# A mixture-of-experts audio tower on one core: the token embedding computed one round ahead, and the value product moved to other PSUM banks

## The reference

```python
# tokenizer: patches of 16 frames, stride 8, x 16 features -> 256; then layernorm with gamma, beta
y = einsum('bpi,di->bpd', patches, W) + b
h = (y - mean) * rsqrt(var + 1e-5) * gamma + beta
# attention on layernorm(h), one head of 256, 124 tokens per sequence, 128 sequences
h = h + softmax((q @ k.T) / scale) @ v
# experts on layernorm(h): router of 6 experts, the best two of each token, gates from a softmax over both
h = h + sum_k gate_k * expert_k(layernorm(h))      # three layers of 256 x 256, relu, relu, none
```

## Time and profile before

| | |
|---|---|
| time, median of 3 runs | 1345.66 us (1345.2 to 1346.94) |
| time of the profiled execution | 1342.78 us |
| its span, first to last instruction | 1341.0 us |
| mean granted TensorE clock | 0.967 |
| busy: PE, weight load, DVE, ACT, POOL | 1234.8, 1078.0, 1062.5, 838.0, 928.3 us |
| part A, until the last round's places | 0 to about 670 us |
| transition | about 670 to 700 us |
| part B | about 700 to 1341 us |

### The profile page before, as it was taken

How to read it: one execution, slowest core, us unless ns; L and a number is a source line. 1 busy time by engine, 2 the same in 40 slices (tenths; PEclk the granted TensorE clock), 3 DMA queues, 4 the chain that set the end, 5 groups by cost and what they waited for, 6 DMA issues and landing times. The chain is left out here.

```text
span 1341.0 us, 28426 instructions
## 1 busy us (share of the span) xinstructions
PE 1234.8 (92%) x7888; PEld 1078.0 (80%) x7888; DVE 1062.5 (79%) x3590; ACT 838.0 (62%) x1838; POOL 928.3 (69%) x740
## 2 busy tenths in 40 slices
PE   3899999999999999999629999999999999999994
PEld 3788888888888888887428788888888888888883
DVE  3589989998999899987547778787787787777873
ACT  1477666766676667766316666766667667666662
POOL 2127778777877787777753677676676676766766
PEclk7899999999999999999759999999999999999997
DMA  2124555544444444445677796667876778778755
GB/s 83 31 63 130 147 131 150 142 115 113 117 124 116 114 116 124 116 114 161 174 204 198 159 225 113 123 122 146 193 120 113 126 154 178 129 146 191 122 63 60
DMA packets 134564, 176.50 MB, mean 132 GB/s; under 512 B 38019, under 2 KB 102406, under 8 KB 134406
## 3 DMA queue, kind: packets, MB, share of 16 engines
q0 software_dynamic: 75456, 69.19, 32.7%
q1 hardware_dynamic: 56822, 101.44, 24.8%
q10 hardware_dynamic: 2128, 4.05, 1.0%
HBM read 168.72 MB, written 101.48 MB: 202 GB/s over the span
## 5 line engine op out<-in xcount | busy, mean ns | idle before, releaser
L533 POOL DMA_INDIRECT out<-yo,tail x268 | 438.7, 1637 | 199.3 <-issue 147.7
L481 POOL DMA_INDIRECT expert_rows<-rec,row_i x256 | 347.6, 1358 | 78.4 <-issue 64.2
L909 ACT ACTIVATE h2v<-bank,small 128x512 f32<-128x512 f32 x134 | 92.4, 690 | 206.9 <-PE bank L725 191.9
L749 PE MATMUL bank<-w_sb,h_hi 128*128 128x256 f32 x1072 | 208.7, 288 | 2.0 <-issue 2.0
L725 PE MATMUL bank<-x_hi,w_sb 128*128 128x512 f32 x536 | 178.2, 393 | 6.3 <-issue 2.7
L725 PE MATMUL bank<-h_hi,w_sb 128*128 128x512 f32 x536 | 177.0, 391 | 1.2 <-DVE h_lo L1229 1.2
L749 PEld LDWEIGHTS bank<-w_sb,h_hi 128*128 128x128 f32 x1072 | 171.3, 191 | 2.8 <-issue 2.7
L749 PE MATMUL bank<-w_sb,h_lo 128*128 128x256 f32 x536 | 151.4, 283 | 0.0
L868 ACT ACTIVATE xn<-h,nmr,rstd 124x256 f32<-124x256 f32 x128 | 66.4, 589 | 126.0 <-DVE nmr L1082 126.0
L725 PEld LDWEIGHTS bank<-x_hi,w_sb 128*128 128x128 f32 x536 | 101.3, 189 | 30.3 <-issue 7.3
L469 POOL TENSOR_TENSOR rstd<-vareps,neghalf 124x4 f32<-124x4 f32 x96 | 114.5, 1192 | 8.0
(11 more groups left out here) (187 smaller groups left out, 3115.0 us busy)
## 6 DMA issues: line engine op xcount, KB each, us to landing
w_sb<-split_weights SPq DMA_DIRECT2D x201, 512.0 KB
xg<-expert_rows SPq DMA_DIRECT2D x67, 530.0 KB
out<-h SPq DMA_DIRECT2D x32, 496.0 KB
small<-in_esmall SPq DMA_DIRECT2D x69, 134.0 KB
split_weights<-half_w SPq DMA_DIRECT2D x36, 256.0 KB
x_in<-in_x SPq DMA_DIRECT2D x32, 250.0 KB
raw_w<-in_eweights SPq DMA_DIRECT2D x36, 128.0 KB
out<-yo,tail POOLq DMA_INDIRECT x268
```

The source lines that it names most:

```text
L481: pool.indirect_dma_start(rows_dram, bass.IndirectOffsetOnAxis(ap=row_i[0:TOK, slot, j, k:k + 1], axis=0), rec[0:TOK, slot, j, :], None).t ...
L533: pool.indirect_dma_start(out, bass.IndirectOffsetOnAxis(ap=tail[:, s, j, E8:].bitcast(I32), axis=0), yo[:, ys, j, :], None, compute_op=AL ...
L749: mm = pe.matmul(banks[6 + b][:, (j % 2) * D:(j % 2 + 1) * D], act[:, c, j * P:(j + 1) * P], w[:, 2, c, wh, :], start=(c == 0 and p == 0), ...
L909: act.activation(h2v[:, m, :], banks[4 + m][:], ACT.Relu, bias=small[:, slot, DC + m:DC + m + 1]).then_inc(S["h2_v"], 1)
```

## The change

It moves stages by a round, and PSUM banks:

* Two rounds, -2 and -1, stand ahead of round 0. The split of the input (xT_hi, xT_lo) is now of group it + 2, and the embedding (PE), its statistics 0 and y (DVE) and their inverse standard deviation (POOL) are of group it + 1. h, statistics 1 and all behind keep their round.
* On ACT the split stands between gexp and qT, on DVE ahead of the weight chunk's lower half. On DVE statistics 0 stand behind nmr of x0, and y behind statistics 2. Input loads go three rounds ahead.
* The value product goes to banks 4 and 3 instead of 6 and 7; waits for banks follow.
* On POOL the power for statistics 1 comes first, then scatters 5 and 6, the power for statistics 0, scatter 7, the power for statistics 2, scatters 0 to 4.
* `fold()` runs on DVE at the end of round 0; PE keeps it behind the embedding, which in round 0 is now that of group 1. The upper and lower halves of the v weights move likewise.
* The constants of POOL are reordered: the two large clears (pad_rows, xg) come last, and the engines wait for smaller counts.

```diff
-            for it in range(G + DEPTH - 1):
+            for it in range(-2, G + DEPTH - 1):
...
-                if it + 1 < G:
-                    load_x(it + 1, (slot_it + 1) % RING)
+                if 2 <= it + 3 < G:
+                    load_x(it + 3)
+                if it < 0:
+                    return
...
@@ gpsimd, step @@
-                if x0:
-                    wait_apart(pool, S["ln1"], g * LN1_N + 2 * GB, S["pool_passed"])
-                    inverse_std(0, S["rstd1"], g)
-                if x5:
-                    scatter(x5[0], range(4, 6))
                 if x0:
                     wait_apart(pool, S["ln1"], g * LN1_N + 6 * GB, S["pool_passed"])
                     inverse_std(1, S["rstd2"], g)
                 if x5:
-                    scatter(x5[0], range(6, 8))
+                    scatter(x5[0], range(5, 7))
+                if xa:
+                    wait_apart(pool, S["ln1"], g * LN1_N + 2 * GB, S["pool_passed"])
+                    inverse_std(0, S["rstd1"], g)
+                if x5:
+                    scatter(x5[0], range(7, 8))
...
-                    scatter(g, range(4 if g < G - 1 else GB * TOPK))
+                    scatter(g, range(5 if g < G - 1 else GB * TOPK))
@@ tensor @@
-            pe.wait_ge(S["pool_const"], 20)
+            pe.wait_ge(S["pool_const"], 16)
...
-                if x0:
-                    g, slot, rnd = x0
+                if xa:
+                    g, slot, rnd = xa
                     pe.wait_ge(S["xT_high"], g + 1)
                     pe.wait_ge(S["xT_low"], g + 1)
...
-                        bank_read(pe, (S["v_ready"], it - 2, (it - 2) * 2 + pair + 1),
-                                  (S["ln1"], it - 1, (it - 1) * LN1_N + 2 * GB + 2 + 2 * pair))
+                        bank_read(pe, (S["ln1"], g - 1, (g - 1) * LN1_N + 2 * GB + 2 + 2 * pair))
...
-                            into = banks[6 + pair][0:TOK, j * D:(j + 1) * D]
+                            into = banks[4 - pair][0:TOK, j * D:(j + 1) * D]
@@ scalar @@
-            act.wait_ge(S["pool_const"], 20)
+            act.wait_ge(S["pool_const"], 2)
...
-                if x0:
-                    act.activation(xT_hi[:], x_in[:, slot, :], ACT.Identity).then_inc(S["xT_high"], 1)
...
                     act.activation(gexp[0:TOK, :], gap[0:TOK, :], ACT.Exp).then_inc(S["gate_exp"], 1)
+                if xs:
+                    wait(act, S["tok_ps"], g * 2)
+                    wait(act, S["xT_low"], g)
+                    act.activation(xT_hi[:], x_in[:, slot, :], ACT.Identity).then_inc(S["xT_high"], 1)
@@ vector @@
-                if x0:
-                    v.tensor_tensor(xT_lo[:], x_in[:, slot, :], xT_hi[:].bitcast(F32), ALU.subtract
-                                    ).then_inc(S["xT_low"], 1)
                 if x4:
                     probabilities(*x4)
...
-                    statistics(0, lambda j: embedded(j), S["ln1"], g * LN1_N, g)
...
-                        v.scalar_tensor_tensor(out=y[R, j, :], in0=embedded(j), scalar=mv[R, 0, j, 0:1],
-                                               in1=gamma_bc[R, :], op0=ALU.subtract, op1=ALU.mult).then_inc(S["ln1"], 1)
...
+                if xs:
+                    v.tensor_tensor(xT_lo[:], x_in[:, slot, :], xT_hi[:].bitcast(F32), ALU.subtract
+                                    ).then_inc(S["xT_low"], 1)
                     v.wait_ge(S["w_high"], it + 1)
...
                     v.scalar_tensor_tensor(out=nmr[R, 0, :], in0=mv[R, 1, :, 0], scalar=-1.0, in1=rstd[R, 1, :],
+                if xa:
+                    statistics(0, lambda j: embedded(j), S["ln1"], g * LN1_N, g)
 ...
+                if xa:
+                    for j in range(GB):
+                        v.scalar_tensor_tensor(out=y[R, j, :], in0=embedded(j), scalar=mv[R, 0, j, 0:1],
+                                               in1=gamma_bc[R, :], op0=ALU.subtract, op1=ALU.mult).then_inc(S["ln1"], 1)
+                if it == 0:
+                    fold()
+                    low_halves("v", 4)
                 if x3:
                     shifted_logits(*x3)
```

More of the change, by code:

```diff
@@ L485, in step @@
             def step(it, group_of):
[L486 to L492 removed]
+                xa, x0, x2, x4, x5 = (group_of(s) for s in (-1, 0, 2, 4, 5))
                 if x0:
@@ L578, in step @@
             def step(it, group_of):
-                x0, x1, x2, x3, x4 = (group_of(s) for s in range(DEPTH))
+                xa, x1, x2, x3, x4 = (group_of(s) for s in (-1, 1, 2, 3, 4))
+                if it == 1:
+                    pe.wait_ge(S["bv_ready"], 1)
                 if x1:
@@ L695, in step @@
                     g, slot, rnd = x1
+                    if it == 1:
+                        pe.wait_ge(S["folded"], 3)
                     for pair in range(2):
-                        bank_read(pe, (S["ln1"], it, it * LN1_N + 2 * GB + 2 + 2 * pair),
-                                  (S["v_ready"], it - 2, (it - 2) * 2 + pair + 1))
+                        if pair == 0:
+                            bank_read(pe, (S["pT_sb"], it - 2, it - 1))
+                        else:
+                            bank_read(pe, (S["pos"], it - 4, (it - 4) * POS_N + 1), (S["xn2T_sb"], it - 3, (it - 3) * 2 + 1),
+                                      (S["v_ready"], it - 2, (it - 2) * 2 + 2))
                         for j in (0, 1):
                             b = 2 * pair + j
-                            into = banks[6 + pair][0:TOK, j * D:(j + 1) * D]
+                            into = banks[4 - pair][0:TOK, j * D:(j + 1) * D]
                             for c in range(DC):
@@ L789, in step @@
             def step(it, group_of):
-                x0, x1, x2, x3, x4 = (group_of(s) for s in range(DEPTH))
-                if x0:
[L792 to L795, removed]
-                    act.activation(xT_hi[:], x_in[:, slot, :], ACT.Identity).then_inc(S["xT_high"], 1)
[L797 to L801, removed]
+                xs, x0, x1, x2, x3, x4 = (group_of(s) for s in (-2, 0, 1, 2, 3, 4))
                 if x4:
@@ L856, in step @@
                     act.activation(rhT[:], banks[5][:, 0:GT], ACT.Relu, bias=rb1_col[:, 0:1]).then_inc(S["rh_sb"], 1)
[L858 to L861, removed]
+                if it >= 0:
+                    slot_it, rnd_it = slot_of(it, group_of)
+                    act.wait_ge(raw_loaded[slot_it], rnd_it * 16 + 16)
+                    wait(act, w_stored[slot_it], rnd_it * 16)
+                    act.activation(half_w[:, slot_it, 0, :], raw_w[:, slot_it, :], ACT.Identity).then_inc(S["w_high"], 1)
                 if x0:
@@ L870, in step @@
                                        ).then_inc(S["xn1_ready"], 1)
+                if it == 0:
+                    act.wait_ge(S["const_loaded"], N_CONST)
+                    high_halves("v")
+                    act.wait_ge(S["fold_sb"], 9)
+                    act.activation(proj["q"][:, 0, :, :], qk_raw[:], ACT.Identity).then_inc(S["proj_high"], 1)
                 if x1:
@@ L875, in step @@
                         act.activation(v_sb[0:TOK, 2 * pair:2 * pair + 2, :],
-                                       banks[6 + pair][0:TOK, :].rearrange("p (b n) -> p b n", b=2),
+                                       banks[4 - pair][0:TOK, :].rearrange("p (b n) -> p b n", b=2),
                                        ACT.Identity).then_inc(S["v_ready"], 1)
@@ L985, in step @@
             def step(it, group_of):
-                x0, x1, x2, x3, x4 = (group_of(s) for s in range(DEPTH))
-                if x0:
-                    g, slot, rnd = x0
-                    v.wait_ge(S["xT_high"], g + 1)
-                    v.tensor_tensor(xT_lo[:], x_in[:, slot, :], xT_hi[:].bitcast(F32), ALU.subtract
-                                    ).then_inc(S["xT_low"], 1)
+                xs, xa, x0, x1, x2, x3, x4 = (group_of(s) for s in range(-2, DEPTH))
                 if x4:
@@ L1073, in step @@
                     v.reciprocal(rinv[R, :], probs[R, :, TOK]).then_inc(S["av"], 1)
[L1075 to L1078, removed]
+                if xs:
+                    g, slot, rnd = xs
+                    v.wait_ge(S["xT_high"], g + 1)
+                    v.tensor_tensor(xT_lo[:], x_in[:, slot, :], xT_hi[:].bitcast(F32), ALU.subtract
+                                    ).then_inc(S["xT_low"], 1)
+                if it >= 0:
+                    slot_it, rnd_it = slot_of(it, group_of)
+                    v.wait_ge(S["w_high"], it + 1)
+                    v.tensor_tensor(half_w[:, slot_it, 1, :], raw_w[:, slot_it, :], half_w[:, slot_it, 0, :].bitcast(F32),
+                                    ALU.subtract).then_inc(S["w_low"], 1)
                 if x0:
@@ L1094, in step @@
                     statistics(2, lambda j: h[R, g % KEPT, j, :], S["av"], at + 1 + GB, g)
+                if xa:
+                    g, slot, rnd = xa
+                    at = g * LN1_N
+                    if it == -1:
```

(13 more changed lines are left out.)

60 lines of the change are left out of this document (27 added, 33 removed).

## The result

| | before | after |
|---|---|---|
| median of 20 runs each | 1345.33 us | 1338.81 us |
| ratio of times (95% interval) | | 0.995 (0.994 to 0.996) |
| profiled execution: time, span | 1342.78, 1341.0 us | 1336.13, 1334.3 us |
| mean granted TensorE clock | 0.967 | 0.969 |

A forecast was written before the change was run, and what follows sets the result against it. A DVE-POOL ring through rstd was taken to hold the 19.11 us round, then one through ACT's half_w; 4.9 from part A's rounds plus 6.0 from the head made 10.9 us gained, 1335 us forecast, range 1316 to 1346.

The forecast's parts named there:

- The round: Rounds 4 to 30 of part A, lshift to lshift: 18.99 us after the change, against 19.11 before.
- the ring as written: Path from lshift through ACT's half_w, DVE's half_w, statistics 0 and y to the next lshift: 18.99 us.
- Round 31: Round without embedding, statistics 0 and y after the change; PE idles 2.11 us before rec's transposes; 16.9 us.
- The head: Start of the kernel up to lshift of round 3: 79.2 instead of 85.25, 6.0 us gained (bounds 3 and 8).
- Behind part A: POOL's closing chain of scatters and DVE's tables shift with round 33; nothing gained or lost there.
- DVE is the only bound: Full rounds: half_w's ring shorter than read, DVE's own work gives 18.36 us a round, 1318 in all; chance 0.12.
- POOL becomes the bound: Full rounds: slower powers and scatters lift POOL from 17.8 to 19.6 us a round, 1351 in all; chance 0.07.
- nothing gained: Rounds and head: a ring of 19.2 and a fold delaying q lose the gain; 1342 to 1347 us; chance 0.13.
- the clock falls each round: Full rounds: an unbroken PE pause lowers its clock, costing 1.2 to 1.9 us each; 1370 to 1385; chance 0.05.

The follow-up runs named there:

- half_act_early: The changed kernel with ACT's half of the weight chunk (half_w) between qT and pT instead of behind rhT; 1306.89 us.
- half_dve_late: The changed kernel with DVE's half of half_w behind y instead of ahead of nmr, ACT untouched; 1314.21 us.
- before_half_early: Control: the kernel before the change, with ACT's half_w moved between qT and pT; 1345.83 us.
- fold_first: The changed kernel with the weight fusing (fold) back ahead of the first h on PE, DVE and ACT; 1337.24 us.
- xt_behind_logits: The changed kernel with ACT's half_w between qT and pT and, from round 3, DVE's xT_lo between lshift and psums; 1300.64 us.
- value_banks_67: The changed kernel with the value product back in banks 6 and 7, its waits adapted; 1483.11 us in one run.

## Why the prediction was right, and where it was not

* **The round: right.** 18.99 was forecast and 18.99 to 19.00 came, by the ring as written, with ACT's half_w at L + 11.28 and DVE's waits of 0.72 and 0.30 (0.65 and 0.3 forecast). half_act_early and half_dve_late open it, and before_half_early shows that it is the change's own.
* **Round 31: off by 0.5, by the path as written.** It took 17.37, for 16.9. PE idles ahead of the transposes of rec, but for 3.52 and not 2.11, behind which the granted clock is 0.57 (599 to 603); DVE comes to half_w at L + 13.30, for 12.92. With 27 rounds of 19.006 that makes the 4.0 gained of 4.9.

```profile
597.85 0.73 PE L632 MATMUL bank<-ident,rec 124*128 124x124 f32 x2 [3.52 <-ACT rec L822]
```

* **The head: the mis-sized term.** 6.0 forecast, 3.8 measured, though within the bounds of 3 to 8. The step that failed is "PE leaves it at 33.3, transposes, embeds group 2 and comes to q at 38.6". PE did leave the fold at 33.4, but the transposes and the embedding took 7.0 us for the 5.3 of that step (PE's timeline):

```profile
30.85 1.86 PE L577 MATMUL bank<-ones_r,qk_raw 128*128 128x1 f32 x8 [3.27 <-DVE qk_raw L987]
...
33.43 1.89 PE L593 MATMUL bank<-ident,xn 124*128 124x124 f32 x8
34.98 0.77 PE L551 MATMUL bank<-tok_proj,xT_hi 128*124 128x256 f32 x2
...
40.42 0.39 PE L551 MATMUL bank<-xn1T_hi,q_proj 128*128 128x496 f32 x1
```

  The transposes took 1.55, where eight that wait for nothing take 0.84 in a full round, and the embedding 5.44, for the 4.65 of the earlier trace rows and 3.40 in a full round before (314.90 to 318.30). The granted clock was 0.50 from 33.0 to 34.8 and 0.58 from 34.8 to 40.4, behind a pause of 3.27 in the fold and small matmuls. q came at 40.42, beyond the upper bound of 39.5 that I had set for the clock; these 1.8 are most of the 2.3 by which L of round 3 came late (81.46 for 79.2). fold_first shows that the fold's new place gains nothing; that the clock alone makes the 1.7 us of these two stages is read from durations and granted clock, and no run isolates it.
* **Behind part A: wrong in two directions.** "Nothing is gained or lost there" left out that rounds 32 to 34 gain 0.9 more, and that part B starts when SP's load of its rows may go. SP's timelines, before and then after:

```profile
678.32 5.46 SPq L372 DMA_DIRECT2D xg<-expert_rows  x2
```

```profile
671.60 3.41 SPq L376 DMA_DIRECT2D xg<-expert_rows  x2
684.50 0.85 SPq L362 DMA_DIRECT2D w_sb<-split_weights  x3
```

  That load is 6.7 earlier, where L of round 34 is 8.6 earlier, and PE's first matmul of part B is 6.5 earlier. The end of POOL's chain of scatters came 7.3 earlier. Why the load gains less than the rounds isn't settled; POOL's last scatter waits 6.0 for a DMA to land in both kernels.
* **The rival "DVE is the only bound"** did not come true in the change, and its 18.36 was no floor. Opened, the round went to 17.8 and, with pexp covered and POOL's work shortened, to 17.4 to 17.6, since 0.4 to 0.54 of DVE's time were scatters, not work. As a forecast for half_act_early it missed by 15 us.
* **The rival "POOL becomes the bound"**: 17.8 for POOL was right in size: in half_act_early and xt_behind_logits it works without a pause, and with its additions left out the 17.72 of the latter fell to about 17.5. It isn't reached in the change. The power that left xT_lo did get shorter (all powers together 1073 ns on average from 250 to 550 us, for 1230 before).
* **The rival "nothing gained"** did not come true: its ring of 19.2 measured 19.0, and q came before today's 40.90, if only by 0.5.
* **The rival "the clock falls each round"** did not come true in the change, where rec comes in pieces and the granted clock is 1.00. value_banks_67 shows the other case: one unbroken pause of 4.75, then 0.50.

The best version run, xt_behind_logits, takes 1300.64 us and computes all that the reference asks: 45 us under before, 38 under the change.

## What to carry to other kernels

After cutting a ring, write down the next one with its margin, and look in it for work that nobody on the path needs: here 0.41 us of half_w cost 32 us of the kernel for its place in ACT's order. Try the cheap edit in the kernel before as well: another split of the scatters alone gained more than a restructuring over five engines. And before an engine's busy time is called its need, look for instructions that take several times their usual length; they can be a wait for another engine that no list of waits shows.

## What was not expected of the hardware

* A small conversion on DVE took 0.71, 0.58 or 0.17 us, an addition 0.43 or 0.14, by where in a scatter's 1.3 to 1.5 us it came; the long ones ended 0.01 to 0.04 us before the scatter. A TENSOR_TENSOR just ahead of a held conversion, under the same scatter, kept its 0.14.
* Behind a pause of 4.75 us in each round PE was granted 0.50 for 2.7 us; behind a pause of 3.52 in round 31 0.57 for 4 us; behind a pause of 3.3 us and small matmuls in the head 0.58 for 5.6 us; with pauses of 0.2 in pieces, 1.00 over 490 us.
